# A newly searched order of 1751 steps in a two-layer transformer kernel

## The chip, the cores and the metric

The kernel runs on one core of one Trainium2 chip. The metric is the device time of one execution in microseconds (us). The core has five engines that run beside each other, each through its own list of instructions in order: PE (TensorE, matrix products and transposes), DVE (VectorE), ACT (ScalarE), POOL (GpSimd) and SP (SyncE, which here only issues DMAs). They wait for each other by semaphores.

## The reference, cut to what matters

Input: eight sequences ("batches" b = 0 to 7) of 512 tokens by 256 features, in float32. Two layers, each an attention part and a feed part, each part fed by a normalised, scaled and shifted input and added back through a gate:

```python
# layer 0
h = layernorm(x) * (1 + ca) + sa
x = x + ga * (h + concat(lin(h), win(h)) @ Wout)   # lin: linear attention on a feature map; win: softmax over a window of 64
h = layernorm(x) * (1 + cb) + sb                    # then mixed with the token before it
x = x + gb * (sigmoid(xr @ W_r) * (square(relu(xk @ W_k)) @ W_v))
# layer 1
h = layernorm(x) * (1 + ca) + sa
x = x + ga * (causal_softmax_attention(rope(h)) @ w_proj + b_proj)
h = layernorm(x) * (1 + cb) + sb
h = silu(h @ w1.T) * (h @ w2.T)
h = gelu(h @ h1.T); h = gelu(h @ h2.T)
x = x + gb * (h @ w3.T)
```

Each attention has 16 heads of 16 features, handled in four "quads" of four heads. The feed part of layer 1 has 1024 hidden features and ternary weights.

## The kernel before

The work is cut into 1751 named steps, `layer:name.numbers`. One table, the string ORDER (L1201 on), lists them, and every engine runs its own part of each step in that listed order; a step in which an engine has no part costs it nothing. So the table fixes five instruction streams at once. The waits are worked out from the steps' names. The PSUM places are dealt out in the listed order too: in layer 0 `lin`, `win` and `wm` steps use the four "wide" banks, and most other steps take turns on two single banks, m0 and m1.

Steps of layer 0 (b is the batch, n = 4b + quad):

- `stats.b` statistics of x (DVE L542, and POOL L448 takes the power); `norm.b`, `rms.b` the normalised input h (`rms` also has SP load the next batch's norm gates); `hT`, `qk`, `v` transpose and project it; `tq.n`, `tk.n` turn queries and keys (DVE L695 keeps the low part of the queries), `fold.n` the feature map.
- `wm.n.0`, `pair.n` (= `wm.n.1` and `lin.n-1.2`) the window's maxima (DVE L705 to L714), `again.n` turns them back; `lin.n.j`, `win.n.j` the weights (PE into a wide fill, then an ACT activation L862, L869, then POOL masks L452, L457); `lv.n.j`, `wv.n.j` the products with the values (PE L1077); `lh.n`, `wh.n` turn the sums back (PE L1087) and divide them (DVE L562 to L567); `turn.b.i`, `out.b.i` the output product. `out.b.i` also has DVE add the result to x, take statistics and, with i = 1, write the second norm xn (L735), and has SP load the gate ga of batch b + 1 (L353).
- `xg.b` on POOL: h *= ga, x += h (L475, L476); it waits for that gate.
- `xT.b.i` turns xn (PE L971); with i = 1, DVE mixes it with the token before (L741, L744, two of each for r, two for k). `r.b.i` and `kk.b.i` are the products of the feed part. `last.b.i` is its last product (PE L1129) and the add into x (DVE L574, L575); SP writes half a batch to x_mid (L398), and after `last.b.1` waits for both halves and loads x of batch b + 3 into the same buffer (L401), which `stats.b+3` reads.
- `wt.i.half` prepares the weights of layer 1: DVE collects low bits (L588) and transposes (L593) a piece that lies in SBUF, SP writes it out (L372) and issues the loads of the piece after next, 16 small DMAs in most steps (L345), 8 in the first few (L350).

Steps of layer 1: `stats`, `norm`, `hT`, `proj` (PE L1908, DVE L1665 to L1678), `tq`, `tk` (PE L1917), `max.b.g.j` (three wide fills a quad, PE L1937; DVE adds the mask L1685 and takes the maxima L1688), `again` (L1924), `att.b.g.j` (PE L1951, L1955, ACT exp L1833 or its like, POOL mask L1607), `values` (L1971), `heads`, `turn`, `out`, `xT`, `split`, and the feed part `up`, `h1`, `h2`, `last` (PE L2012, L2028, L2042). The attention of batch b + 1 is laid between the feed steps of batch b. "The seam" below is the stretch in which the last batch of layer 0 and the first attention of layer 1 run together, before any feed step of layer 1 can be laid between.

Of the kernel before, what the change touches and what calls it, by code (L numbers as in the profile page):

```python
# [1201 lines left out]
0:stats.0 0:norm.0 0:wturn.0.0 0:mod0.0 0:hT.0.0 0:masks.0 0:hT.0.1 0:rows.0.0 0:rms.0 0:qk.0.0 0:qk.0.1 0:qk.0.2 0:wt.0.0 0:qk.0.3 0:v.0.0 0:tq.0  # L1202
0:xg.0 0:tk.0 0:wturn.0.1 0:wm.0.0 0:tk.1 0:tk.2 0:wturn.0.2 0:tq.1 0:pair.0 0:fold.0 0:fold.1 0:wt.0.1 0:wm.1.0 0:mod.0 0:lin.0.0 0:again.0 0:lin.0.1
0:v.0.1 0:pair.1 0:stats.1 0:wt.1.0 0:tq.2 0:lv.0.0 0:again.1 0:win.0.0 0:lv.0.1 0:fold.2 0:win.0.1 0:tq.3 0:lin.1.0 0:lv.0.2 0:wv.0.0 0:rows.0.1
0:wt.1.1 0:win.1.0 0:wv.0.1 0:tk.3 0:lv.1.0 0:norm.1 0:wm.2.0 0:hT.1.0 0:hT.1.1 0:wv.1.0 0:win.1.1 0:rms.1 0:lh.0 0:wh.0 0:wt.2.0 0:lin.1.1 0:qk.1.0
0:wv.1.1 0:pair.2 0:v.1.0 0:again.2 0:lin.2.0 0:fold.3 0:lv.1.1 0:wt.2.1 0:lin.2.1 0:qk.1.1 0:win.2.0 0:lv.1.2 0:qk.1.2 0:wm.3.0 0:qk.1.3 0:lv.2.0
0:pair.3 0:wt.3.0 0:tk.4 0:lh.1 0:wv.2.0 0:lin.3.0 0:wh.1 0:tq.4 0:lv.2.1 0:wt.3.1 0:win.2.1 0:again.3 0:lv.2.2 0:lin.3.1 0:tq.5 0:lh.2 0:win.3.0
0:wv.2.1 0:lv.3.0 0:fold.4 0:turn.0.0 0:wm.4.0 0:v.1.1 0:turn.0.2 0:pair.4 0:wv.3.0 0:tk.5 0:lv.3.1 0:win.3.1 0:wt.4.0 0:stats.2 0:fold.5 0:lv.3.2
0:lin.4.0 0:wh.2 0:wv.3.1 0:lh.3 0:again.4 0:lin.4.1 0:wh.3 0:turn.0.1 0:turn.0.3 0:wt.4.1 0:wm.5.0 0:out.0.0 0:pair.5 0:out.0.1 0:tk.6 0:win.4.0
0:lv.4.0 0:xg.1 0:tq.6 0:lv.4.1 0:win.4.1 0:again.5 0:lv.4.2 0:lin.5.0 0:wt.5.0 0:fold.6 0:tq.7 0:win.5.0 0:lh.4 0:wv.4.0 0:lin.5.1 0:wv.4.1 0:tk.7  # L1210
0:xT.0.0 0:norm.2 0:wm.6.0 0:hT.2.0 0:hT.2.1 0:lv.5.0 0:rms.2 0:pair.6 0:wh.4 0:qk.2.0 0:wt.5.1 0:again.6 0:lin.6.0 0:wt.6.0 0:wv.5.0 0:lv.5.1
0:xT.0.1 0:lv.5.2 0:win.5.1 0:qk.2.1 0:lin.6.1 0:qk.2.2 0:lv.6.0 0:win.6.0 0:fold.7 0:qk.2.3 0:wm.7.0 0:tk.8 0:r.0.0 0:tq.8 0:pair.7 0:v.2.0 0:wv.5.1
0:lv.6.1 0:win.6.1 0:lh.5 0:again.7 0:lv.6.2 0:lin.7.0 0:wh.5 0:tk.9 0:wv.6.0 0:wt.6.1 0:wv.6.1 0:lin.7.1 0:kk.0.0 0:fold.8 0:win.7.0 0:kk.0.1 0:tq.9
0:win.7.1 0:lv.7.0 0:lh.6 0:wm.8.0 0:lv.7.1 0:v.2.1 0:pair.8 0:r.0.1 0:again.8 0:wv.7.0 0:lv.7.2 0:win.8.0 0:wh.6 0:wt.7.0 0:last.0.0 0:wv.7.1
0:lin.8.0 0:last.0.1 0:lh.7 0:wm.9.0 0:turn.1.2 0:turn.1.0 0:wv.8.0 0:wh.7 0:tq.10 0:lin.8.1 0:turn.1.1 0:wt.7.1 0:lv.8.0 0:turn.1.3 0:tq.11 0:pair.9
0:fold.9 0:out.1.0 0:lin.9.0 0:wt.8.0 0:out.1.1 0:lin.9.1 0:lv.8.1 0:tk.10 0:win.8.1 0:again.9 0:tk.11 0:wm.10.0 0:lv.8.2 0:xg.2 0:xT.1.0 0:fold.10
0:wv.8.1 0:lh.8 0:pair.10 0:stats.3 0:lv.9.0 0:lv.9.1 0:xT.1.1 0:lin.10.0 0:again.10 0:lv.9.2 0:win.9.0 0:r.1.0 0:win.9.1 0:lv.10.0 0:win.10.0
# [956 lines left out]
```

## Time and profile before

| | |
|---|---|
| median of 3 runs | 1990.87 us (1989.52 to 1991.04) |
| profiled execution, its own time | 1990.24 us |
| its span, first to last instruction | 1988.5 us |
| PE busy | 1866.2 us (94%) |
| DVE, ACT, POOL busy | 68%, 45%, 26% |
| mean granted clock of PE | 0.972 |
| chain that ended last | PE 74%, DVE 14%, ACT 5%, issue 3% |

The profile gives busy time by engine; what an engine waited for; a timeline; and windows with the granted clock of PE (1.00 is 2.4 GHz, 0.50 is 1.2 GHz). A row of the timeline is: start in us from the start of the span, duration in us, engine, line, operation, tiles written and read, shapes, number of merged instructions, and in brackets the idle time of the engine before it and what ended it.

### The profile page before, as it was taken

Reading aid. Unit: us, or ns where it says so; the run is one execution under the profiler, and the core shown is the slowest. Engines: PE = TensorE matmul, PEld = TensorE weight load, DVE = VectorE, ACT = ScalarE, POOL = GpSimd, SP = SyncE. Lnnn points to the kernel's source line nnn. Section 1 sums busy time; section 2 is a strip of 40 time slices with the busy share of each in tenths; the row PEclk is TensorE's granted clock in tenths of the full one; section 3 lists DMA queues with packets and bytes.
Section 4 is the critical chain, followed back from the end, with each engine's and each line's share of the span. In section 5 each row is a group of like instructions: output and inputs, shape, how many; then the busy total and the mean of one; then the engine's idle time right before and its main releaser. Section 6 shows DMA issues by size and latency. Waiting matters only on the chain.

```text
span 1988.5 us, 40531 instructions
## 1 busy us (share of the span) xinstructions
PE 1866.2 (94%) x16217; PEld 1308.3 (66%) x16217; DVE 1359.8 (68%) x2382; ACT 904.1 (45%) x1134; POOL 509.0 (26%) x597
## 2 busy tenths in 40 slices
...
DMA packets 171818, 126.36 MB, mean 64 GB/s; under 512 B 113944, under 2 KB 148720, under 8 KB 171248
## 3 DMA queue, kind: packets, MB, share of 16 engines
...
q8 instruction: 133, 2.18, 0.5%
q14 instruction: 53, 0.43, 0.1%
q10 hardware_dynamic: 832, 0.01, 0.0%
...
## 4 chain that ended last, share of the span: by engine, by line
PE 74%; DVE 14%; ACT 5%; issue 3%; SPq 1%; POOL 1%; DMA 1%; DVEq 0%; ACTq 0%; POOLq 0%
PE ps L2028 24%; PE ps L2012 4%; PE ps L1077 4%; PE ps L1908 3%; PE ps L1971 3%; PE ps L982 3%; PE ps L2042 3%; PE ps L1937 3%; DVE b_maxima L1688 3%; PE ps L1951 2%; PE ps L1107 2%; PE ps L1955 2%; PE ps L1040 2%; PE ps L1022 2%; PE ps L1129 2%
## 5 line engine op out<-in xcount | busy, mean ns | idle before, releaser
L2028 PE MATMUL ps<-b_acts,b_hidden_w 128*128 128x512 f32 x2048 | 504.4, 399 | 0.7 <-DVEq L1769 0.7
L2028 PEld LDWEIGHTS ps<-b_acts,b_hidden_w 128*128 128x128 f32 x2048 | 376.3, 188 | 92.1 <-issue 12.9
L452 POOL TENSOR_SCALAR_AFFINE_SELECT a_probs<-a_probs 128x512 f32<-128x512 f32 (+1 forms) x224 | 166.1, 757 | 374.0 <-ACT a_probs L862 249.5
L1607 POOL TENSOR_SCALAR_AFFINE_SELECT b_work<-b_work 128x512 f32<-128x512 f32 x128 | 82.4, 657 | 659.6 <-ACT b_work L1833 659.5
L862 ACT ACTIVATE a_probs<-ps 128x2048 f32<-128x2048 f32 (+1 forms) x96 | 153.1, 1595 | 141.6 <-DVEq L712 104.8
L1865 ACT ACTIVATE b_acts_exact<-ps,c_s 128x512 f32<-128x512 f32 x128 | 88.2, 689 | 273.6 <-PE ps L2028 273.3
L1833 ACT ACTIVATE b_work<-ps 128x2048 f32<-128x2048 f32 (+1 forms) x96 | 153.3, 1596 | 88.5 <-PE ps L1955 87.0
L1688 DVE TENSOR_REDUCE b_maxima<-ps 128x4 f32<-128x2048 f32 (+3 forms) x128 | 187.8, 1488 | 3.3
L1778 DVE CAST b_acts<-b_acts_exact 128x512 fp32r<-128x512 f32 x128 | 60.5, 473 | 166.0 <-ACT b_acts_exact L1865 165.7
L1077 PE MATMUL ps<-a_probs,c_va 128*17 128x192 f32 (+4 forms) x2048 | 134.3, 380 | 4.7 <-issue 2.2
L1685 DVE TENSOR_TENSOR ps<-ps,c_causalr 128x512 f32<-128x512 f32 x128 | 86.1, 695 | 43.3 <-PE ps L1937 41.6
L1615 POOL TENSOR_TENSOR b_acts<-b_acts_exact,b_acts 128x512 fp32r<-128x512 f32 x64 | 82.3, 1285 | 126.9 <-DVE b_acts L1773 126.9
L1937 PE MATMUL ps<-c_k_split,c_q_split 32*128 32x512 f32 (+3 forms) x1024 | 68.0, 362 | 25.8 <-DVE b_maxima L1688 13.6
L1779 DVE TENSOR_TENSOR b_acts<-b_acts_exact,b_acts 128x512 fp32r<-128x512 f32 x128 | 88.6, 692 | 4.4
L1971 PE MATMUL ps<-b_work,c_va 128*17 128x512 f32 (+3 forms) x1024 | 87.5, 450 | 2.4 <-POOL b_work L1607 2.4
L1908 PE MATMUL ps<-c_wqkv,b_work 128*128 128x512 f32 (+1 forms) x256 | 85.9, 487 | 0.4 <-ACTq L876 0.4
L1077 PEld LDWEIGHTS ps<-a_probs,c_va 128*17 128x17 f32 x2048 | 46.9, 97 | 58.7 <-issue 43.1
L1937 PEld LDWEIGHTS ps<-c_k_split,c_q_split 32*128 32x128 f32 x1024 | 42.0, 190 | 60.0 <-issue 23.1
L1861 ACT ACTIVATE b_acts_exact<-ps,c_s 128x512 f32<-128x512 f32 x64 | 44.0, 688 | 82.0 <-PE ps L2012 80.3
L2012 PE MATMUL ps<-b_acts,b_w1T 128*128 128x512 f32 x256 | 74.4, 412 | 4.8 <-DVEq L1769 4.1
L1951 PEld LDWEIGHTS ps<-b_shift,c_shift_rows 32*128 32x128 f32 x1280 | 46.3, 184 | 45.8 <-issue 21.0
L2012 PE MATMUL ps<-b_acts,b_w2T 128*128 128x512 f32 x256 | 75.6, 418 | 0.6 <-DVEq L1786 0.6
...
## 6 DMA issues: line engine op xcount, KB each, us to landing
b_hidden_w<-turned_h SPq DMA_DIRECT2D x128, 512.0 KB, 3.5
a_raw_next<-in_L_ffn_h_w SPq DMA_DIRECT2D x512, 16.0 KB, 1.8
...
```

The lines of the kernel that those rows point to most:

```text
L452: return nc.gpsimd.affine_select(out=z, in_=z, compare_op=ALU.is_ge, fill=0.0, base=0, pattern=[[0, blocks_n], [1, cols]], channel_multipl ...
L862: nc.scalar.activation(pb, here[:, :, o:o + w], ACT.Square, bias=1.0, scale=0.5).then_inc(att_ready, 1)
L1077: ins = nc.tensor.matmul(here[R * i:R * i + HD + 1, kb * P:kb * P + q], va[:, b % 2, kb, 4 * g + i, :], pb[:, first + i * pitch:first + i ...
L1688: ins = nc.vector.tensor_reduce(maxima[:, t, :].unsqueeze(2), room["wide"][:, :, o:o + (t + 1) * P], AX.X, ALU.max, negate=True)
L1779: nc.vector.tensor_tensor(dst[:, 1], z, dst[:, 0].bitcast(F32), ALU.subtract).then_inc(h_split, 1)
L1833: ins = nc.scalar.activation(probs[nth % 2][:, 0:4 * w].rearrange("p (h q) -> p h q", q=w), here[:, :, 0:w], ACT.Exp, scale=float(HD) ** -0.5)
L1865: nc.scalar.activation((exact_a if name == "h2" else exact_b)[:, m], here, ACT.Gelu, scale=s12[:, 2 + (name == "h2"), m:m + 1]).then_inc(g ...
L1908: ins = nc.tensor.matmul(here[:, a, 0:w], hT[:, k, t * P:(t + 1) * P], wqkv[:, k, o:o + w], start=(k == 0), stop=(k == ND - 1))
L1937: ins = nc.tensor.matmul(here[:, i, o:o + (t + 1) * P], part[rows_of(i), g % 2, t * P:(t + 1) * P], ksplit[rows_of(i), g % 2, 0:(t + 1) * ...
L1971: ins = nc.tensor.matmul(room["acc"][R * i:R * i + HD + 1, kb * P:S], va[:, kb, 4 * g + i, :], probs[nth % 2][:, i * w + o:i * w + o + S - ...
L2012: ins = nc.tensor.matmul(here, view((w1T, w2T)[j][:, i, k]), view(h2r[:, k, part]), start=(k + part == 0), stop=(k == ND - 1 and part == 1))
L2028: ins = nc.tensor.matmul(here, view(hidden_w[:, m, k]), view(src[:, k, i]), start=(k + i == 0), stop=(k == NHID - 1 and i == 1))
```

## The change

The string ORDER is replaced by another listing of the same 1751 steps. No operation, no wait and no buffer is changed; only the places of steps in the list (and with them which of m0 and m1 a step of layer 0 gets). The steps from `1:xT.7` on stand as before. 127 lines of the table differ; two of them, those around the load of the fifth batch:

```diff
@@ -1199,133 +1199,133 @@
...
-0:last.1.0 0:lin.11.1 0:wt.9.1 0:last.1.1 0:wh.10 0:wm.12.0 0:tk.13 0:turn.2.2 0:lv.11.0 0:fold.12 0:tq.13 0:pair.12 0:wv.11.0 0:lh.10 0:v.3.0
...
+0:wt.9.1 0:tk.12 0:win.11.0 0:wv.10.1 0:last.1.0 0:tk.13 0:wm.12.0 0:lv.11.0 0:lv.11.1 0:fold.12 0:tq.13 0:win.11.1 0:wv.11.0 0:lh.10 0:pair.12
+0:wh.10 0:last.1.1 0:fold.13 0:wm.13.0 0:wv.11.1 0:again.12 0:turn.2.2 0:lv.11.2 0:wh.11 0:turn.2.0 0:lin.12.0 0:lh.11 0:v.3.0 0:wt.10.0 0:win.12.0
...
```

Place 1, SP, around `last.1.0` and `last.1.1`. Before: the write-out and the loads of `wt.9.0`, the first half of x, `wt.9.1` with its 16 loads, the second half and the load of batch 4.

```order
L372 DMA turned_h<-a_staged 128x512
L345 DMA a_raw_next<-in_L_ffn_h_w 32x4x32 x16
L398 DMA x_mid<-a_x 128x2x256
L372 DMA turned_h<-a_staged 128x512
L345 DMA a_raw_next<-in_L_ffn_h_w 32x4x32 x16
L398 DMA x_mid<-a_x 128x2x256
L401 DMA a_x<-in_L_attn_x 128x4x256
```

Now:

```order
L372 DMA turned_h<-a_staged 128x512
L345 DMA a_raw_next<-in_L_ffn_h_w 32x4x32 x16
L372 DMA turned_h<-a_staged 128x512
L345 DMA a_raw_next<-in_L_ffn_h_w 32x4x32 x16
L398 DMA x_mid<-a_x 128x2x256 x2
L401 DMA a_x<-in_L_attn_x 128x4x256
```

Both `wt` steps now stand ahead of both halves, and the load of batch 4 follows the second half at once.

Place 2, POOL, around `xg.4` (L475, L476). Before, the mask of `lin.17.2` (the one L452 row right above) stands ahead of it:

```order
L448 TENSOR_TENSOR a_rstd<-a_vareps,c_minus_half 128x4
L452 AFFINE_SELECT a_probs<-a_probs 128x4x128 x4
L457 AFFINE_SELECT a_probs<-a_probs 128x4x128
L452 AFFINE_SELECT a_probs<-a_probs 128x4x128
L475 TENSOR_TENSOR a_h<-a_h,a_ga 128x1024
L476 TENSOR_TENSOR a_x<-a_x,a_h 128x1024
L452 AFFINE_SELECT a_probs<-a_probs 128x8x128
```

Now `xg.4` is ahead of that mask, and so earlier:

```order
L448 TENSOR_TENSOR a_rstd<-a_vareps,c_minus_half 128x4
L452 AFFINE_SELECT a_probs<-a_probs 128x4x128 x2
L457 AFFINE_SELECT a_probs<-a_probs 128x4x128
L452 AFFINE_SELECT a_probs<-a_probs 128x4x128 x2
L475 TENSOR_TENSOR a_h<-a_h,a_ga 128x1024
L476 TENSOR_TENSOR a_x<-a_x,a_h 128x1024
L452 AFFINE_SELECT a_probs<-a_probs 128x4x128 x2
```

`xg.3` goes the other way. Before, it stands behind the masks of `win.12.1` (L452 x4 and L457), ahead of that of `lin.13.2`:

```order
L452 AFFINE_SELECT a_probs<-a_probs 128x4x128 x4
L457 AFFINE_SELECT a_probs<-a_probs 128x4x128
L475 TENSOR_TENSOR a_h<-a_h,a_ga 128x1024
L476 TENSOR_TENSOR a_x<-a_x,a_h 128x1024
L452 AFFINE_SELECT a_probs<-a_probs 128x4x128
L452 AFFINE_SELECT a_probs<-a_probs 128x8x128
```

Now the mask of `lin.13.2` is the last of the three rows merged above it:

```order
L452 AFFINE_SELECT a_probs<-a_probs 128x4x128 x2
L457 AFFINE_SELECT a_probs<-a_probs 128x4x128
L452 AFFINE_SELECT a_probs<-a_probs 128x4x128 x3
L475 TENSOR_TENSOR a_h<-a_h,a_ga 128x1024
L476 TENSOR_TENSOR a_x<-a_x,a_h 128x1024
L452 AFFINE_SELECT a_probs<-a_probs 128x4x128
```

So `xg.3` now starts right ahead of `xT.2.1`, in the same pattern (`pair`, `wh`, `wt`, `xT.b.1`) in which `xg.4` stood before.

Place 3, PE, the first attention quad of layer 1 in the seam. L1937 x8 of 512 columns is `max.0.0.0`, the next two L1937 rows are `max.0.0.1`. Before:

```order
L1040 MATMUL ps<-a_mT,c_k_split 128x256 x8
L1937 MATMUL ps<-c_k_split,c_q_split 128x512 x8
L1937 MATMUL ps<-c_k_split,c_q_split 128x384 x8
L1937 MATMUL ps<-c_k_split,c_q_split 128x128 x8
L1917 MATMUL ps<-c_identr,c_nat 128x128 x4
L1077 MATMUL ps<-a_probs,c_va 17x512 x4
L1917 MATMUL ps<-c_identr,c_nat 128x128 x4
L1077 MATMUL ps<-a_probs,c_va 17x384 x4
L1077 MATMUL ps<-a_probs,c_va 17x128 x4
L1937 MATMUL ps<-c_k_split,c_q_split 128x256 x8
L1937 MATMUL ps<-c_k_split,c_q_split 128x512 x8
```

Now:

```order
L1040 MATMUL ps<-a_mT,c_k_split 128x256 x8
L1937 MATMUL ps<-c_k_split,c_q_split 128x512 x8
L1917 MATMUL ps<-c_identr,c_nat 128x128 x8
L1077 MATMUL ps<-a_probs,c_va 17x512 x4
L1937 MATMUL ps<-c_k_split,c_q_split 128x384 x8
L1937 MATMUL ps<-c_k_split,c_q_split 128x128 x8
L1129 MATMUL ps<-a_wrT,a_mix 128x256 x4
L1937 MATMUL ps<-c_k_split,c_q_split 128x256 x8
```

Between the first and the second fill of that quad now stand two turns (L1917) and one product with values (L1077) where nothing stood; between the second and the third stands one product (L1129) instead of two turns and three products.

## Rows read from the trace of the kernel before

**Rows 1.** The page: busy us of each engine, share of the span, instructions.

```profile
PE 1866.2 (94%) x16217; PEld 1308.3 (66%) x16217; DVE 1359.8 (68%) x2382; ACT 904.1 (45%) x1134; POOL 509.0 (26%) x597
```

**Rows 2.** Windows: length, busy PE, PEld, DVE, ACT, POOL, clock, DMA share, GB/s.

```profile
100.00:700.00 600.00, 564.79 (x6182) 374.11 (x6181) 417.88 (x750) 350.46 (x463) 243.01 (x289) 0.97 0.22 51
700.00:1000.00 300.00, 254.90 (x2390) 164.22 (x2392) 214.88 (x369) 123.30 (x142) 72.36 (x89) 0.93 0.13 45
1000.00:1900.00 900.00, 886.19 (x6619) 650.11 (x6620) 635.23 (x1067) 371.90 (x441) 153.67 (x166) 1.00 0.25 73
```

**Rows 3.** Timeline of the DMA queue around the fifth batch's load: start, us, what.

```profile
310.05 8.41 SPq L345 DMA_DIRECT2D a_raw_next<-in_L_ffn_h_w  x16
318.50 0.43 SPq L398 DMA_DIRECT2D x_mid<-a_x  x1
320.71 0.39 SPq L401 DMA_DIRECT2D a_x<-in_L_attn_x  x1
```

**Rows 4.** Timeline of DVE and of POOL: first instruction behind a transfer.

```profile
324.65 1.41 DVE L542 BATCH_NORM_STATS2 a_stats<-a_x 128x6 f32<-128x256 f32 x4 [4.86 <-DMA a_x<-in_L_attn_x]
...
417.79 1.41 DVE L542 BATCH_NORM_STATS2 a_stats<-a_x 128x6 f32<-128x256 f32 x4 [3.18 <-DMA a_x<-in_L_attn_x]
...
259.56 2.37 POOL L475 TENSOR_TENSOR a_h<-a_h,a_ga 128x1024 f32<-128x1024 f32 x1 [5.03 <-DMA a_ga<-gate_rows]
```

**Rows 5.** Timeline of PE behind those three transfers.

```profile
265.06 1.05 PE L1077 MATMUL ps<-a_probs,c_va 128*17 128x256 f32 x8 [2.09 <-POOL a_probs L452]
...
327.39 0.66 PE L1087 MATMUL ps<-c_identr,a_sums 128*128 128x128 f32 x4 [1.33 <-DVEq L684]
...
331.68 1.06 PE L1077 MATMUL ps<-a_probs,c_va 128*17 128x192 f32 x24 [1.36 <-issue]
...
420.70 0.66 PE L1087 MATMUL ps<-c_identr,a_sums 128*128 128x128 f32 x4 [1.71 <-DVE a_onat L567]
```

**Rows 6.** Timeline of POOL and of DVE, collision of the fourth batch.

```profile
455.77 2.38 POOL L475 TENSOR_TENSOR a_h<-a_h,a_ga 128x1024 f32<-128x1024 f32 x1
455.85 5.08 DVE L741 TENSOR_SCALAR a_mix<-a_xT,a_one_mu 128x512 f32<-128x512 f32 x2
```

**Rows 7.** Timeline of DVE, the same work undisturbed, and the other collision.

```profile
754.74 0.88 DVE L741 TENSOR_SCALAR a_mix<-a_xT,a_one_mu 128x512 f32<-128x512 f32 x2 [0.73 <-ACT a_xT L898]
...
634.68 2.03 DVE L735 SCALAR_TENSOR_TENSOR a_xn<-a_x,a_meanvar,a_rstd 128x256 f32<-128x256 f32 x4 [1.12 <-POOL a_rstd L448]
...
539.96 4.90 DVE L735 SCALAR_TENSOR_TENSOR a_xn<-a_x,a_meanvar,a_rstd 128x256 f32<-128x256 f32 x4 [1.12 <-POOL a_rstd L448]
...
544.78 2.83 DVE L588 SCALAR_TENSOR_TENSOR a_lows<-a_raw_next,a_lows 128x512 int32<-128x512 int32 x1
```

**Rows 8.** Timeline of PE at both collisions.

```profile
452.37 0.66 PE L1087 MATMUL ps<-c_identr,a_sums 128*128 128x128 f32 x4
...
463.60 2.90 PE L1129 MATMUL ps<-a_wrT,a_mix 128*128 128x256 f32 x6 [4.14 <-DVE a_mix L744]
...
548.86 1.12 PE L971 MATMUL ps<-c_identr,a_xn 128*128 128x128 f32 x4 [4.20 <-DVE a_qlow L695]
```

**Rows 9.** Windows at the lower clock, columns as in rows 2.

```profile
264.60:271.20 6.60, 6.14 (x51) 4.66 (x52) 5.08 (x8) 2.52 (x3) 3.27 (x4) 0.50 0.01 2
421.60:424.80 3.20, 3.20 (x44) 2.41 (x44) 0.88 (x4) 1.43 (x2) 1.07 (x2) 0.50 0.18 28
547.90:554.50 6.60, 5.58 (x34) 4.01 (x38) 4.86 (x8) 1.36 (x2) 0.79 (x2) 0.50 0.27 65
```

**Rows 10.** Timeline of PE at the seam: four stalls.

```profile
789.00 1.33 PE L1937 MATMUL ps<-c_k_split,c_q_split 32*128 32x384 f32 x16 [3.13 <-DVE b_maxima L1688]
...
853.01 0.55 PE L1951 MATMUL ps<-b_shift,c_shift_rows 32*128 32x128 f32 x12 [2.03 <-ACTq L1836]
...
895.46 0.66 PE L1917 MATMUL ps<-c_identr,c_nat 128*128 128x128 f32 x4 [2.65 <-DVE c_nat L1678]
...
936.30 0.51 PE L1937 MATMUL ps<-c_k_split,c_q_split 32*128 32x256 f32 x8 [2.18 <-DVE b_maxima L1688]
```

More of the change, by code:

```diff
@@ L1201 @@
 ORDER = """
[L1202 to L1217, printed above, removed]
```

235 lines of the change are left out of this document (125 added, 110 removed).

## The prediction

> **What bounds the kernel now.** I read the busy times of the page first: PE is busy for 1866.2 of 1988.5 us [rows 1]. No operation changes, so its work stays. What an order can move is the rest, 122 us, and the stretches in which PE runs at the lower clock. Then the windows by stage: layer 0 (100 to 700 us) has PE idle for 600 - 564.8 = 35.2 us at a mean clock of 0.97; the seam (700 to 1000) for 300 - 254.9 = 45.1 us at 0.93; the 900 us after it for 13.8 us at 1.00 [rows 2]. So the long stage in which feed steps fill every hole has nothing to give, and setup and tail stand nearly as before. The place to look is layer 0 and the seam. Next, the waits that end on a DMA, then the timeline of PE for every idle time over 1 us, each followed back to what was late. Three causes show in layer 0.
>
> First, transfers that were issued late. The load of batch 4 should follow the second half of x to x_mid. SP had just begun the 16 small loads of `wt.9.1`, which took 8.41 us of its time; the half went out at 318.50 and the load at 320.71 [rows 3]. DVE, which meets `stats.4` in its fixed order, then stood idle for 4.86 us; the same with batch 5, 3.18 us; and POOL waited 5.03 us for a gate ga behind the loads of `wt.8.0` [rows 4]. On PE this came out as 2.09, then 1.33 + 1.36, then 1.71 us of idle time [rows 5].
>
> Second, collisions of POOL and DVE. While POOL ran `xg.4` (its first half, L475, 2.38 us), the first two L741 of the mix took 5.08 us [rows 6]; alone they take 0.88 [rows 7]. `r.3.0` came 4.14 us late on PE [rows 8]. In batch 4 `xg.5` met xn: four L735 took 4.90 us in place of 2.03, and the L588 behind them 2.83 [rows 7]; `tq.23`, behind that, gave its bank back late, and `xT.4.0` waited 4.20 us [rows 8].
>
> Third, the clock: behind three of these stalls the granted clock is 0.50 (1.2 GHz) for 6.6, 3.2 and 6.6 us, with PE busy before them at 1.00 (2.4 GHz) up to the stall [rows 9].
>
> **The change part by part.** It removes and adds nothing and moves nearly everything a little. The two lists have the same shape: each batch's projections, output products and feed steps begin within some 15 us of PE work of their old places. I therefore price only the places that stalled, and those that have become thinner than places that stalled.
>
> 1. Transfers. In the new order no `wt` with 16 loads stands within 9 us of PE work ahead of any `last.b.1` or `out.b.1`; before, the nearest stood 2 to 4 us ahead in the three cases above. `stats.b` now stands 17 us of PE work or more behind the step that frees its buffer (before, 11.0 and 11.6 in the two cases that stalled; out of the queue it needs the 2.2 us between 318.50 and 320.71 and 3.9 to the landing before 324.65 [rows 3, 4]). Moved past SP's other work, the `wt` steps come no closer to each other than 12 us for the same half, against 8.41 for its loads. So these waits go: 2.09 + 1.33 + 1.36 + 1.71 = 6.5 us. Bounds: 0 if other waits stand right behind them, 13.1 if the whole of DVE's and POOL's idle time (4.86 + 3.18 + 5.03) comes back. I take 6.5, which PE itself shows.
>
> 2. Collisions. `xg.5` now also has the mask of `lin.21.1` and the power of `stats.6` ahead of it on POOL, so it starts some 3 us later, behind xn: minus 4.2 us. `xg.4` is now ahead of `lin.17.2` and runs before the mix: minus 4.1 us. But `xg.3` has been moved behind the mask of `lin.13.2` and `wt.11.1`, exactly the pattern in which `xg.4` collided. From the product before (`wh.16` at 452.37) to `r.3.0` at 463.60 were 11.2 us, 4.14 of them idle [rows 8]; the new list has the same steps there but for one turn and one short product, less one turn, some 0.6 us less work, so `r.2.0` should wait 4.14 + 0.6 = 4.7 us. Net of the three: -4.2 - 4.1 + 4.7 = -3.6 us. Bounds: -8.3 (the new collision does not come) and +0.6 (`xT.4.0` still waits).
>
> The two engines met within 0.1 us of each other (455.77 and 455.85) [rows 6], and the one that came second paid. The Trainium skill (SBUF — State Buffer, "Who interferes with whom") says that the shared pair of ports is an exclusive lock and that issue order, not the operation, decides who blocks. By that, in the new place DVE may as well win, and then POOL would wait for 0.4 us and PE for nothing; this is one reason for a rival below.
>
> 3. Clock. The three stretches at 0.50 are 16.4 us long [rows 9]. Work that runs at half speed there would take half of it, so at most 8.2 us come back; their PE rows are not all limited by the clock, and other holes may set off others. I take half, 4.1 us. Bounds 8.2 back and 3.3 lost (one more stretch of 6.6 us). The one behind `r.3.0` I let move to `r.2.0`.
>
> 4. The seam. With nothing between `max.0.0.0` and `max.0.0.1`, PE waited 3.13 us for DVE's maxima [rows 10]; now 2 us of work stand there: -2.0. `att.0.0.1` now follows `att.0.0.0` at once; where that was so before, it cost 2.03 us [rows 10]: +2.0. Between a second and a third max fill (2.18 us idle with 2.1 us of work between [rows 10]) six places of layer 1 now have at most 2.5 us of work, before four: two more at some 2 us: +4.0 (the fill right behind the one just named is one of them, 1.9 us in place of 3.0). A first and second fill of the third quad have 2.2 us between them in place of 4.3: +1. The first `tk` of batch 1 (2.65 us idle [rows 10]) has 0.9 us more ahead of it: -1.0. Sum +4. Bounds -5 (the old stalls there merge with new ones) and +13 (all six thin fills pay in full, in a row).
>
> 5. Everything else. By the same tally a handful of pairs elsewhere in both layers are thinner than any that ran free before: `values.4.0.2` 0.9 us behind its weights, three turns of sums 0.5 us behind their copies, `xT.3.0` and `xT.6.0` some 5 us behind `out`. I put 3 us on all; bounds 0 and 6.
>
> Sum: -6.5 - 3.6 - 4.1 + 4 + 3 = -7.2 us. Against the profiled execution's own 1990.24 us that is 1983.0; the median of the runs lies 0.6 us above it, so 1983.5.
>
> **The rivals.**
>
> A larger gain: DVE wins the port at `xg.3` or the two miss each other (-4.7), and the stalls of the seam only change places (-4): -7.2 - 8.7 = -15.9, 1975 us. For it: the times of the two engines there differ by less than I can tell. Against: the list repeats the old pattern, and the seam has real thin spots.
>
> No difference: the idle time is kept and only changes its place. DVE is busy for 418 of 600 us in layer 0 and 215 of 300 in the seam [rows 2], waits of different kinds lie side by side, and filling one takes work from another. Then of step 1 half remains, of the clock nothing: -3.3 - 3.6 + 4 + 3 = 0, 1990 us.
>
> Slower: the seam. A PE that waits for every max fill and every weights fill runs in bursts there; the clock of 0.93 over 300 us means 42 us of it at half speed already [rows 2]. If all six thin fills pay 2.2 us each (+13 in place of +4) and these holes keep the clock down for another 20 us (+10), the sum is -7.2 + 9 + 10 = +12, 2002 us; the point from which it decides is about 7 us of idle time and clock lost in the seam beyond my 4. For it: the clock there falls behind stalls of only 1 to 3 us. Against: the largest of them, 3.13 us, is filled.
>
> That the new list does not do what its name says I rule out: the SP rows show the loads out of the way.
>
> **How the numbers follow.** Chances: forecast 0.45 (own range 1978 to 1988), larger gain 0.19, no difference 0.20, slower 0.16. What a measurement of this kernel can tell from no change is 0.2%, 4 us: faster means under 1986.9. Of the forecast 0.41 lies there, all of the larger gain, 0.02 of the third: 0.62. Within 4 us: 0.04 + 0.17 = 0.21. Slower: 0.16 + 0.01 = 0.17. The range 1970 to 1996 takes in the larger gain, no difference, and of the slower case its near part.
>
> **What would show it.** DVE has no idle time that ends on the load of a_x, POOL at most one, in the setup, on a_ga. No idle time of 4 us at `r.3.0` and `xT.4.0`; one of 4 to 5 at `r.2.0`, with an L741 pair of some 5 us beside L475. PE idle from 100 to 700 us at 26 us or less, from 700 to 1000 at 45 to 50, mean clock 0.975 or so. The forecast is wrong if the window from 700 to 1000 us holds 7 us more idle time or its clock falls under 0.90, or if layer 0 keeps its 35 us with other names on it.

## The result and the profile after

| | us, median | runs |
|---|---|---|
| before | 1990.95 | 20 |
| after | 1994.72 | 20 |

The ratio is 1.0022 (95% interval 1.0012 to 1.0032): slower by 0.22%, where 0.4% faster was forecast. The profiled execution of after took 1992.53 us, 2.2 us under the median of its runs, so what its trace shows of the loss (2.3 us against before's own 1990.24) is a little less than the loss of the medians. Every execution of every run below is counted but one: of run 14's twelve, one took 3645.85 us and is left out of its ratio.

Two details of the change: the table has 1750 entries, and behind `1:xT.7` two of them, `split.7` and `last.6.1.0`, have changed places too. Nothing below rests on either.

The busy line of the page, columns as in [rows 1]:

```profile
PE 1865.9 (94%) x16217; PEld 1305.2 (66%) x16217; DVE 1358.6 (68%) x2382; ACT 910.8 (46%) x1140; POOL 509.8 (26%) x597
```

PE's busy time is the same to 0.3 us. The windows, as in [rows 2], show that this sum hides two opposite changes:

```profile
100.00:700.00 600.00, 568.44 (x6310) 376.38 (x6310) 424.72 (x764) 353.84 (x467) 246.59 (x295) 0.99 0.21 49
700.00:1000.00 300.00, 251.26 (x2252) 162.57 (x2250) 212.24 (x356) 117.00 (x136) 67.57 (x83) 0.90 0.14 47
1000.00:1900.00 900.00, 884.25 (x6625) 646.88 (x6624) 628.30 (x1064) 378.77 (x445) 153.54 (x165) 1.00 0.25 73
```

Layer 0 has 31.6 us of PE idle time (35.2 before) and its mean clock rose from 0.97 to 0.99; the seam has 48.7 (45.1) and its clock fell from 0.93 to 0.90; the 900 us behind have 15.8 (13.8).

The transfers of [rows 3, 4] are out of the way. The timeline of the DMA queue at the load of batch 4, and the first work of DVE behind it, which has no idle time:

```profile
317.95 3.28 SPq L345 DMA_DIRECT2D a_raw_next<-in_L_ffn_h_w  x7
321.27 1.77 SPq L398 DMA_DIRECT2D x_mid<-a_x  x2
325.07 0.37 SPq L401 DMA_DIRECT2D a_x<-in_L_attn_x  x1
...
334.00 1.40 DVE L542 BATCH_NORM_STATS2 a_stats<-a_x 128x6 f32<-128x256 f32 x4
```

The collisions of [rows 6, 8] are gone at `xg.4` and `xg.5`, and the new one came at `xg.3` as worked out: POOL's L475 began 0.08 us ahead of DVE's pair of L741, which then took 5.06 us, and `r.2.0` waited 4.00 us on PE (4.7 forecast):

```profile
354.01 2.36 POOL L475 TENSOR_TENSOR a_h<-a_h,a_ga 128x1024 f32<-128x1024 f32 x1
354.09 5.06 DVE L741 TENSOR_SCALAR a_mix<-a_xT,a_one_mu 128x512 f32<-128x512 f32 x2
...
361.83 1.62 PE L1129 MATMUL ps<-a_wrT,a_mix 128*128 128x256 f32 x3 [4.00 <-DVE a_mix L744]
```

In the seam the thin fills wait as the four of [rows 10] did. The timeline of PE at `max.0.0.2`, `att.0.0.1`, `max.1.2.2` and, behind the seam, `max.2.2.2`:

```profile
789.43 0.51 PE L1937 MATMUL ps<-c_k_split,c_q_split 32*128 32x256 f32 x8 [1.87 <-DVE b_maxima L1688]
...
804.50 0.55 PE L1951 MATMUL ps<-b_shift,c_shift_rows 32*128 32x128 f32 x12 [2.03 <-ACTq L1836]
...
953.97 0.51 PE L1937 MATMUL ps<-c_k_split,c_q_split 32*128 32x256 f32 x8 [1.68 <-DVE b_maxima L1688]
...
1094.31 0.51 PE L1937 MATMUL ps<-c_k_split,c_q_split 32*128 32x256 f32 x8 [2.34 <-DVE b_maxima L1688]
```

To compare two orders step by step I matched PE's instructions to the steps, and took from the time of a milestone (the end of a step that stands at nearly the same place in both lists) the nominal work of all steps listed before it, each step at the median of its kind in before. What is left is idle time and slowness (PE busy for longer than nominal). The slowness is an estimate, good to about 1 us. The last column is the time at 0.50 in the record of the granted clock:

| stretch | idle, before and after | slowness, before and after | clock at 0.50 |
|---|---|---|---|
| start to `last.5.1` (714 us) | 53.3, 50.2 | 9.4, 1.3 | 61.4, 40.9 |
| to `up.0.7.1` (965 us) | 44.7, 48.4 | 16.8, 24.7 | 40.9, 58.1 |
| to the last step | 18.7, 20.9 | 5.7, 5.6 | 6.8, 3.4 |

(The clock's column is by time: up to 700 us, 700 to 1000, and from 1000 to PE's last instruction.) Layer 0 won 11.2 us, 8.1 of them slowness; the second stretch lost 11.6, 7.9 of them slowness; the rest lost 2.1. The second stretch is more than the seam. The experiments below cut the lists just ahead of `up.0.2.0` (some 930 us), where both have the same steps behind them: up to there the same reckoning gives a loss of 6.7 us (2.3 idle, 4.4 slowness), from there to `up.0.7.1` 5.1 (1.5 and 3.6). Time at 0.50 went down by 20.5 us, then up by 17.2, and half of such time is lost work: 10.2 and 8.6 us, beside 8.1 and 7.9 of slowness. So the clock accounts for the slowness in both stretches, and the idle time moved less. Over the whole kernel the two clock shares cancel: slowness 31.9 us before and 31.6 after, idle time 116.7 and 119.5.

### The profile page after: what moved, and what is told of

It reads as the page before. It is cut to its first block, busy times and chain, and to the rows that moved or that the text cites. A ratio compares the mean times of both kernels' runs of the same rounds, so it can differ in the third digit from the quotient of the medians.

```text
span 1990.8 us, 40537 instructions
## 1 busy us (share of the span) xinstructions
PE 1865.9 (94%) x16217; PEld 1305.2 (66%) x16217; DVE 1358.6 (68%) x2382; ACT 910.8 (46%) x1140; POOL 509.8 (26%) x597
## 4 chain that ended last, share of the span: by engine, by line
PE 78%; DVE 14%; ACT 4%; issue 2%; POOL 0%; DMA 0%; SPq 0%; DVEq 0%; ACTq 0%; POOLq 0%
PE ps L2028 24%; PE ps L2012 5%; PE ps L1077 4%; PE ps L1908 4%; PE ps L1971 3%; PE ps L982 3%; PE ps L2042 3%; PE ps L1937 3%; PE ps L1951 2%; PE ps L1955 2%; PE ps L1107 2%; PE ps L1022 2%; PE ps L1040 2%; DVE b_maxima L1688 2%; PE ps L1129 2%
## 5 line engine op out<-in xcount | busy, mean ns | idle before, releaser
L452 POOL TENSOR_SCALAR_AFFINE_SELECT a_probs<-a_probs 128x512 f32<-128x512 f32 (+1 forms) x224 | 166.2, 758 | 357.5 <-ACT a_probs L862 249.0
L1778 DVE CAST b_acts<-b_acts_exact 128x512 fp32r<-128x512 f32 x128 | 55.8, 436 | 171.9 <-ACT b_acts_exact L1865 171.6
L1077 PE MATMUL ps<-a_probs,c_va 128*17 128x192 f32 (+4 forms) x2048 | 135.3, 385 | 2.9 <-issue 1.6
L1685 DVE TENSOR_TENSOR ps<-ps,c_causalr 128x512 f32<-128x512 f32 x128 | 86.2, 696 | 50.2 <-PE ps L1937 48.2
L1937 PE MATMUL ps<-c_k_split,c_q_split 32*128 32x512 f32 (+3 forms) x1024 | 68.4, 363 | 29.5 <-DVE b_maxima L1688 13.6
L1077 PEld LDWEIGHTS ps<-a_probs,c_va 128*17 128x17 f32 x2048 | 47.9, 98 | 58.6 <-issue 39.8
L1937 PEld LDWEIGHTS ps<-c_k_split,c_q_split 32*128 32x128 f32 x1024 | 42.0, 191 | 62.9 <-issue 23.4
L457 POOL TENSOR_SCALAR_AFFINE_SELECT a_probs<-a_probs 128x1024 f32<-128x1024 f32 (+2 forms) x96 | 74.7, 794 | 4.4
```

The lines of the kernel that those rows point to most:

```text
L452: return nc.gpsimd.affine_select(out=z, in_=z, compare_op=ALU.is_ge, fill=0.0, base=0, pattern=[[0, blocks_n], [1, cols]], channel_multipl ...
L1077: ins = nc.tensor.matmul(here[R * i:R * i + HD + 1, kb * P:kb * P + q], va[:, b % 2, kb, 4 * g + i, :], pb[:, first + i * pitch:first + i ...
L1937: ins = nc.tensor.matmul(here[:, i, o:o + (t + 1) * P], part[rows_of(i), g % 2, t * P:(t + 1) * P], ksplit[rows_of(i), g % 2, 0:(t + 1) * ...
```

## The experiments

Each run is a re-listing of the same steps. "Old" is the list before, "new" the list after. Differences in us are differences of ratio times 1991; a single ratio is good to 0.1 or 0.2%, so a difference of two of these runs has some 3 to 5 us on either side.

**Runs 1 to 3: which stretch of the list loses.**

```diff
-new
+run 1: new[:722] + what is left, in old order
+run 2: new[:901] + what is left, in old order
+run 3: old[:722] + what is left, in new order
```

> The list is the new one up to the end of batch 5 (its first 722 entries, last step a first half of last.5), and the steps left stand in their old order: new layer 0, old seam, old layer 1. Theory A, the seam's own order is the loss: in the two profiles the new list is 11.2 us ahead at last.5.1, and from there the old order should keep it: 1991 - 11 = 1980 us, ratio 0.994 to 0.995; window 700:1000 with 43 to 47 us of PE idle time and a clock of 0.92 to 0.93, as before. Theory B, what layer 0 wins the seam gives back whatever its order (the granted clock there falls when more work was done before it, or the products of the seam wait for something that layer 0 does not move): 1990 to 1995 us, clock in the seam 0.90 or 0.91.

> The new list up to step up.0.1.1 of layer 1 (about 935 us), the old order behind it: it prices the new order of the long stage of layer 1 alone. Theory A: the profiles were 1.8 us apart in favour of the new one at 925 us and 2.5 us against it at the end, so the rest of the new list costs some 4 us: 1991 - 2 = 1989 us, ratio 0.999. Rival: that 4 us is run-to-run noise or a late effect of the seam and stays: 1994 us, as the whole new list, ratio 1.002.

> The reverse of the first: old order up to the end of batch 5 (722 entries), the steps left in their new order. Theory A (the loss lies in the new seam and the new layer 1): 1991 + 11 (what the seam lost by 1000 us) + 3 (behind it) = 2005 us, ratio 1.006 to 1.008; window 700:1000 with 48 us or more of PE idle and a clock of 0.90. Theory B (the loss is the answer to a faster layer 0): about 1991 us, ratio 1.000 to 1.001, with the seam's clock at 0.93.

Measured: run 1 1986.85 us, ratio 0.9976 (0.9964 to 0.9988); run 2 1987.12 us, 0.9976 (0.9966 to 0.9985); run 3 2005.6 us, 1.0072 (1.0057 to 1.0087). Run 3 is as theory A said: new seam and new layer 1 cost 14 us on an old layer 0, and since the whole new list stands at 1.0022, the new layer 0 is worth 10. Run 1 is between the theories. Its trace points to the reason: the lead of 9.8 us at `last.5.1` fell to 5.3 at `out.6.1`, at the joint of the two orders, where `win.28.1` and `win.29.0` waited 1.66 and 1.52 us as in neither list. A joint has a price of its own. Run 2 against the whole new list gives 9 us (give or take 3) for the new order behind 934 us; I had 4, and the trace of after shows 7 there. Runs 1 and 2 have the same ratio, so behind the new layer 0 the new seam cost nothing, or 4.5 us if run 1's joint is taken off; on a repaired old layer 0 it cost 7 (run 11).

**Run 4: the collision at `xg.3`, moved later.**

```diff
-0:xg.3 0:xT.2.1 0:lv.13.0 0:lin.14.0 0:lv.13.1 0:again.14 0:win.13.0 0:lh.12 0:r.2.0
+0:xT.2.1 0:lv.13.0 0:lin.14.0 0:lv.13.1 0:again.14 0:win.13.0 0:lh.12 0:r.2.0 0:xg.3
```

> The whole new list with one step moved: xg.3 stands behind r.2.0, and so behind the mix of xT.2 on DVE, in place of ahead of xT.2.1. Theory C, the collision of POOL's L475 with DVE's first L741 pair (5.06 us in the new profile, r.2.0 4.00 us late on PE, 3.4 us at the lower clock behind it) is what that place costs: r.2.0 has no idle time, the L741 pair takes about 0.9 us, -4.0 - 1.7 = -5.7: 1994.7 - 5.7 = 1989 us, ratio to the kernel before 0.999. Rival: POOL's two instructions of 4.8 us now meet other work of DVE (L665 of the next batch's h), which is stretched as much, and PE waits there: 1993 to 1995 us, ratio 1.001 to 1.002.

Measured: 1997.53 us, ratio 1.0031 (1.002 to 1.0042). The collision went (the first L741 pair took 0.84 us, `r.2.0` had no idle time) and a wait took its place, which neither theory named (the rival had `L665` stretched, not waiting). DVE's next norm writes a_h, and must wait until POOL has read it; in time order:

```profile
363.52 2.36 POOL L475 TENSOR_TENSOR a_h<-a_h,a_ga 128x1024 f32<-128x1024 f32 x1
365.96 2.37 POOL L476 TENSOR_TENSOR a_x<-a_x,a_h 128x1024 f32<-128x1024 f32 x1
368.44 3.53 DVE L665 SCALAR_TENSOR_TENSOR a_h<-a_x,a_meanvar,a_hg 128x256 f32<-128x256 f32 x4 [6.91 <-POOL a_x L476]
373.34 1.72 PE L971 MATMUL ps<-c_identr,a_h 128*128 128x128 f32 x4 [4.84 <-DVE a_h L669]
```

DVE stood idle for 6.91 us and `hT.4.0` on PE for 4.84, more than the 4.00 that had been won.

**Runs 5 to 7: the terms of the prediction, one by one, in the old list.**

```diff
 run 5
-0:wt.9.1 0:last.1.1            -0:wt.13.0 0:lin.15.1 0:last.2.1   -0:wt.8.0 0:out.1.1
+0:last.1.1 0:wt.9.1            +0:lin.15.1 0:last.2.1 0:wt.13.0   +0:out.1.1 0:wt.8.0
 run 6
-0:pair.18 0:xg.4               -0:xg.5 0:wt.17.1 0:lin.21.1
+0:xg.4 0:pair.18               +0:wt.17.1 0:lin.21.1 0:xg.5
 run 7: both
```

> The old list with three steps moved by a few places: wt.9.1 right behind last.1.1, wt.13.0 right behind last.2.1, wt.8.0 right behind out.1.1. So no step with 16 loads stands ahead of a load of a_x or of that of a_ga. It prices the first term of the prediction alone. Theory A (the waits go, nothing stands behind them): DVE's 4.86 and 3.18 us and POOL's 5.03 us of idle time gone; PE wins the 6.5 us of its own, and with the lower clock behind two of these stalls (6.6 and 3.2 us at 0.50, so up to 4.9) 6.5 to 11: 1991.5 - 8.5 = 1983 us, ratio 0.995 to 0.997. Rival (other waits stand right behind them): 0 to 2 us, ratio 0.999 to 1.000.

> The old list with two steps moved: xg.4 ahead of pair.18 (POOL idle there for 8 us), xg.5 behind lin.21.1, one mask later. It prices the removal of the two collisions alone. Theory A: r.3.0 and xT.4.0 lose their 4.14 and 4.20 us of PE idle time and the two stretches of 6.8 us at the lower clock behind them go (6.8): -8.3 - 6.8 = -15 us at most, 1991.5 - 12 = 1980 us, ratio 0.993 to 0.996. Rival: POOL's pair of 4.8 us meets other work of DVE that reads and writes SBUF only, as in the run in which xg.3 stood behind r.2.0 and another step waited 4.84 us: 0 to -5 us, ratio 0.998 to 1.001.

> The old list with both of the two edits before: five steps moved, all else as before. If the terms add, the gains of the two runs add up: 1991.5 - 8.5 - 12 = 1971 us, ratio 0.988 to 0.991, half-clock time between 400 and 700 us at 7 us or less against 23.9. If idle time only changes its place (the rival of no difference), the sum is less than the larger of the two: ratio 0.995 or above. The seam is in its old order, 700:1000 at a clock of 0.92 to 0.93: if it gives back what layer 0 wins whatever its order, the ratio is 0.996 or above too, and the lead at the end of layer 0 is 5 us or more larger than that at the end.

Measured: run 5 1980.36 us, ratio 0.9939 (0.9919 to 0.9959); run 6 1984.79 us, 0.9963 (0.995 to 0.9976); run 7 1975.31 us, 0.9923 (0.9903 to 0.9943). So the two repairs are worth 12, 7 and together 15 us: more, less and less than theory A had, and in no case what the rival had. Within their intervals the terms add, and five moved steps beat both kernels.

What came back was not the idle time. PE's window from 100 to 700 us in run 5 (columns as in [rows 2]):

```profile
100.00:700.00 600.00, 565.09 (x6244) 373.07 (x6244) 422.19 (x756) 355.37 (x466) 243.91 (x292) 0.98 0.22 51
```

PE is idle for 34.9 us, where before had 35.2: the waits of 2.09, 1.33 and 1.36 us are gone, as forecast, and waits of 3.75, 1.16 and 1.35 us have come: what the rival said of idle time, though not its price. The trace is 5.5 us ahead at `last.5.1` all the same, with 13.6 us less at 0.50. In run 7 the 14.2 us of lead there are 4.9 of idle time and 9.3 of slowness, where terms 1 and 2 for these places were 14.8 of idle time. In run 6 `xT.4.0` waited 0.75 us in place of 4.20, but `r.3.0` still 2.56: `xg.4` is earlier only as far as its gate's transfer allows. In run 7 the trace's lead was still 13.2 us at `up.0.7.1`. The old seam gives next to nothing back (5.5 and 5.4 in run 5, 6.3 and 6.6 in run 6), so theory B of run 1 has fallen.

Removing a wait can uncover a collision. In run 5 the gate for `xg.2` came in time, POOL started earlier, beside DVE's xn, and the L588 behind it took 2.86 us; in time order:

```profile
253.03 3.15 DVE L735 SCALAR_TENSOR_TENSOR a_xn<-a_x,a_meanvar,a_rstd 128x256 f32<-128x256 f32 x4 [1.13 <-POOL a_rstd L448]
255.88 2.54 POOL L475 TENSOR_TENSOR a_h<-a_h,a_ga 128x1024 f32<-128x1024 f32 x1
256.11 2.86 DVE L588 SCALAR_TENSOR_TENSOR a_lows<-a_raw_next,a_lows 128x512 int32<-128x512 int32 x1
...
261.89 0.69 PE L1022 MATMUL ps<-a_bandr,c_identr 128*128 128x192 f32 x4 [3.75 <-DVE a_maxima L707]
```

PE waited 3.75 us there, where 2.09 had been [rows 5].

**Run 8: a place for `xg.3` that works.** On the list of run 2:

```diff
-0:pair.14 0:wh.12 0:wt.11.1 0:xg.3      -0:xT.6.0 0:lv.29.2
+0:xg.3 0:pair.14 0:wh.12 0:wt.11.1      +0:lv.29.2 0:xT.6.0
```

> The list of the second run (new up to 920 us, old behind it) with two steps moved: xg.3 ahead of pair.14, one mask earlier, when the new norm has been long read and the mix has not begun; xT.6.0 behind lv.29.2, 1.1 us later. If the collision at r.2.0 (4.00 us of idle time, 3.4 to 6.8 us at the lower clock) goes without the wait of the next norm that cost the gain in the fourth run: -4 - 2.5; at xT.6.0 the idle time of 1.96 us halves and with it the 6.8 us at the lower clock: -1 to -4. Sum some -8: 1987 - 8 = 1979 us, ratio 0.993 to 0.995. Rival (POOL's pair delays the masks that lh.12 and the feed's products wait for by 2 to 4 us): ratio 0.997 to 0.998, as the second run.

Measured: 1979.71 us, ratio 0.9945 (0.9926 to 0.9964), against 0.9976 for run 2, so -6 us; I had -8. `r.2.0` on PE:

```profile
359.57 2.90 PE L1129 MATMUL ps<-a_wrT,a_mix 128*128 128x256 f32 x6 [1.43 <-DVE a_mix L744]
```

The wait is down from 4.00 to 1.43 us. The other edit did not do what I expected: the lower clock behind `xT.6.0` lasted 6.8 us as before.

**Run 9: the price of a thin fill, ten times.** A fill is thin when too little work of PE stands ahead of it to cover what it waits for. On the list of run 7, for example:

```diff
-1:max.2.0.1 1:tk.2.1 1:h2.0.3.1 1:h2.0.4.0 1:max.2.0.2
+1:max.2.0.1 1:h2.0.3.1 1:max.2.0.2 1:tk.2.1 1:h2.0.4.0
```

> The list of the seventh run (old with five steps moved, ratio 0.9923) with ten third max fills of layer 1 put forward: in the quads 0 and 3 of batches 2 to 6 one product of the feed, 2.0 us, is left between max.b.g.1 and max.b.g.2, where 2.7 to 5.1 us stood. All ten lie between 1000 and 1700 us, where PE has no idle time of that kind and runs at 1.00. It prices a thin fill. Theory D (idle time and clock): each waits about 1.9 us as the thin fills of the new list did (1.68, 1.78, 1.87, 2.03, 2.34 us), and behind most of them the granted clock is 0.50 for 3.4 us, 1.7 us more: 10 x 3.6 = 36 us at most, 1975 + 25 to 36 = 2000 to 2011 us, ratio 1.004 to 1.009. Rival (idle time only): 1975 + 19 = 1994 us, ratio 1.001 to 1.002, mean clock 0.977 or more, as the seventh run.

Measured: 2001.89 us, ratio 1.0056 (1.0041 to 1.007): 26.5 us more than run 7, which is theory D and excludes the rival's 19. All ten fills waited, nine of them 1.77 or 1.78 us and one 1.63. The timeline of PE at the first and the last, and the windows around them (length, busy PE, clock, DMA share, GB/s):

```profile
1023.88 0.51 PE L1937 MATMUL ps<-c_k_split,c_q_split 32*128 32x256 f32 x8 [1.77 <-DVE b_maxima L1688]
...
1684.25 0.51 PE L1937 MATMUL ps<-c_k_split,c_q_split 32*128 32x256 f32 x8 [1.77 <-DVE b_maxima L1688]
```

```profile
1022.00:1030.00 8.00, 6.23 (x38) 1.00 0.21 66
1682.00:1690.00 8.00, 6.23 (x27) 0.79 0.11 18
```

The same stall left the clock at 1.00 once, and set it to 0.50 for 3.4 us the other time. From `up.0.7.1` to the last step, idle time rose by 16.7 us and slowness by 8.8, with 17 us more at 0.50, in five stretches of 3.4. Only three of the five stretches stood behind thin fills; two stood behind stalls of 1.39 and 1.75 us which run 7 has too, without a drop. So a stall of 1.77 us cost (16.7 + 8.8) / 10 = 2.6 us on the mean; a third of the price is the clock, and the stall alone does not say where it falls.

**Runs 10 and 11: the two parts of the new list on a clean one.** On the list of run 7:

```diff
+run 10: run 7[:901] + what is left, in new order
+run 11: run 7[:722] + entries 722 to 900 in new order + the rest in old order
```

> The list of the seventh run for its first 901 entries (up to step up.0.1.1 of layer 1, some 920 us), the new order behind it. It prices the last part of the new list with a layer 0 and a seam that are clean. In the profile of the new list this part lost 4.3 us against before, 2.34 of them at max.2.2.2, 1.57 and 1.68 at again.1.1 and max.1.2.2. Theory A (local): 1975 + 4 to 7 = 1980 us, ratio 0.994 to 0.996. Rival (the part costs nothing by itself): 1975 us, ratio 0.992 to 0.993.

> The list of the seventh run, but with its entries 722 to 900 in their new order (some 715 to 920 us); behind them the old order again. It prices the new seam alone, with its thin fills. In the traces with the new seam this stretch lost 9 to 12 us against the old one, 5 of them from xT.6.0 to hT.0 and 4 between max.0.2.2 and att.0.3.2, half as idle time, half as time at the lower clock. Theory A (local): 1975 + 10 = 1985 us, ratio 0.996 to 0.998, half-clock time between 700 and 1000 us 50 us or more against 44 in the seventh run. Rival (the first and the second run had the same ratio, so the new seam costs nothing): 1975 to 1977 us, ratio 0.992 to 0.993.

Measured: run 10 1984.14 us, ratio 0.9954 (0.9937 to 0.9971), 6 us over run 7; run 11 1981.98 us, 0.9959 (0.9941 to 0.9977), 7 us over it. Each part costs by itself (each difference has 5 us on either side), and their sum of 13 agrees with run 3's 14. The windows 700:1000 of run 7 and of run 11 (columns as in [rows 2]):

```profile
700.00:1000.00 300.00, 255.31 (x2331) 164.31 (x2330) 215.59 (x366) 121.22 (x143) 70.48 (x85) 0.93 0.14 47
```

```profile
700.00:1000.00 300.00, 253.84 (x2294) 164.28 (x2293) 212.25 (x359) 121.06 (x141) 71.19 (x84) 0.91 0.14 47
```

By steps, from `last.5.1` to `up.0.7.1`, run 11 had only 1.4 us more idle time than run 7 (45.8 and 44.4), but 5.3 us more slowness (23.3 and 18.0), and 54.7 us at 0.50 in place of 44.4. The new seam hardly waits longer, it waits at other places. Over all traces, the time at 0.50 between 700 and 1000 us was 41 to 44 us in the eight that have the old seam behind an old or repaired layer 0 (54.6 in run 1), and 55 to 68 in the whole new list and runs 3, 4, 11 and 14. But run 2 had 48 and run 8, also with the new order up to 934 us, only 38: one profile of one list does not fix it.

**Run 12: the one repair that the new seam made, alone.** On the list of run 7:

```diff
-1:max.0.0.0 1:max.0.0.1 1:tk.0.1 0:lv.31.0
+1:max.0.0.0 1:tk.0.1 0:lv.31.0 1:max.0.0.1
```

> The list of the seventh run with max.0.0.1 moved behind lv.31.0: 2 us of work between the first and the second max fill of the first quad, where nothing stood and PE waited 3.13 us. It is the one repair that the new seam made, alone. Theory A: idle time of 3.13 us gone, at max.0.1.0 perhaps 0.5 more, one stretch of the lower clock (6.8 us) shorter: 1975 - 3 to - 5 = 1971 us, ratio 0.990 to 0.991. Rival (DVE's chain of maxima bounds the whole quad, the idle time only moves on to max.0.0.2 and max.0.1.0): 1975 us, ratio 0.992 to 0.993, with idle times there of 2 us and more.

Measured: 1976.22 us, ratio 0.9922 (0.9906 to 0.9939), the same as run 7: the rival. The timeline of PE at `max.0.0.1`, `max.0.0.2` and `max.0.1.0`:

```profile
778.75 0.80 PE L1937 MATMUL ps<-c_k_split,c_q_split 32*128 32x384 f32 x16 [1.56 <-DVE b_maxima L1688]
783.34 0.80 PE L1937 MATMUL ps<-c_k_split,c_q_split 32*128 32x256 f32 x8 [2.21 <-DVE b_maxima L1688]
786.26 1.23 PE L1937 MATMUL ps<-c_k_split,c_q_split 32*128 32x512 f32 x8 [2.12 <-DVEq L1693]
```

3.13 us at the first became 1.56 there and 2.21 at the second, and a wait of 1.15 us at `max.0.1.1` went. From `max.0.0.1` to `max.0.1.1` that makes 5.9 us of idle time, where run 7 has 6.4: a filler here shifts the wait, because DVE's maxima bound the quad.

**Runs 13 and 14: what was open.**

```diff
 run 13, on run 7: wt.8.0 back
-0:out.1.1 0:wt.8.0
+0:wt.8.0 0:out.1.1
 run 14, on the whole new list: xg.3 as in run 8, and
-1:max.1.2.2 1:values.1.1.1 1:up.0.5.1 1:att.1.1.2 1:again.1.2 1:up.0.6.0 1:up.0.6.1
+1:values.1.1.1 1:up.0.5.1 1:att.1.1.2 1:max.1.2.2 1:up.0.6.0 1:up.0.6.1 1:again.1.2
-1:max.2.2.2 1:up.1.3.1 1:tk.2.3 1:up.1.4.0 1:again.2.2 1:values.2.1.2 1:ga.2 1:up.1.4.1
+1:up.1.3.1 1:tk.2.3 1:up.1.4.0 1:max.2.2.2 1:values.2.1.2 1:ga.2 1:up.1.4.1 1:again.2.2
```

> The list of the seventh run with wt.8.0 back in its old place (four steps moved in place of five). There the load of a_ga for xg.2 comes late again. Theory E (that wait was cover: without it POOL's L475 starts at 251.7 us beside DVE's xn and the L588 behind it takes 2.85 us, so wm.10.1 waits 3.73, win.9.0 1.15 and wh.8 1.35 us where only lv.9.2 had waited 2.09): 6.2 - 2.1 = 4 us less idle time, 1975 - 4 = 1971 us, ratio 0.990 to 0.991, one stall of 2 us at lv.9.2 again. Rival (the wait and the collision cost the same): 1975 us, ratio 0.992 to 0.993.

> The whole new list with five steps moved: xg.3 ahead of pair.14 (as in the eighth run), and the two thin fills behind 934 us filled: max.1.2.2 behind att.1.1.2, max.2.2.2 behind up.1.4.0, with again.1.2 and again.2.2 a little later. Theory A (the losses are these places): -6 for the collision (ratios 0.9945 against 0.9976 in the eighth and second run, less a little for xT.6.0), -1.7 - 2.3 of idle time and 3 of 3.4 us stretches at the lower clock, -5: 1995 - 6 - 9 = 1980 to 1984 us, ratio 0.995 to 0.997. Rival (the loss behind 934 us is spread over the stage, not in these two fills): only the collision's 4 to 6 us come back: 1989 to 1991 us, ratio 0.999 to 1.000.

Measured: run 13 1975.9 us, ratio 0.993 (0.991 to 0.9951), no different from run 7: the rival again. The trace does show the stalls change as theory E said (`lv.9.2` 2.25 us, 0.36 at `wm.10.1` for 3.73), and idle time up to `last.5.1` is 3.6 us less, but the time at 0.50 there is 3.4 us more, and the medians are the same within what six executions tell. Run 14 1993.38 us, ratio 1.0013 (0.9999 to 1.0026): theory A has fallen, and the run cannot be told from the new list itself. The timeline of PE behind the fill that I moved, at `up.1.4.0` and `again.2.2`:

```profile
1092.46 1.19 PE L2012 MATMUL ps<-b_acts,b_w1T 128*128 128x512 f32 x4 [1.43 <-DVEq L1769]
...
1097.98 0.30 PE L1924 MATMUL ps<-c_identr,c_kT 128*128 128x128 f32 x1 [2.21 <-DVE c_kT L1697]
```

The 2.34 us at `max.2.2.2` are gone, and 1.43 + 2.21 have come. Moving a late step later made the step that follows it thin. Nor did the whole of run 14 show the 6 us of run 8: its trace is 3 us ahead of after's at `last.5.1`, and level with it at the end.

## Why the prediction was wrong

Its steps, against what was measured:

1. Transfers, -6.5 us. All three waits went, with no DVE idle time on a_x. Alone in the old list they were worth 12 us (run 5, interval 8 to 16), 8 in its trace: the sum of terms 1 and 3 there. Right in that the waits went; wrong in what came back, since run 5's idle time in layer 0 is the same and its whole gain there is slowness. That it came to more than 6.5 was not worked out.

2. Collisions, -3.6 net. `xg.4` and `xg.5` free, `r.2.0` 4.00 us late for 4.7. Right in mechanism, place and size of the stalls. The loser was again the engine that came second, by 0.08 us, so the doubt from the Trainium skill (SBUF — State Buffer, "Who interferes with whom": an exclusive lock, issue order decides) was to the point, and here the trace agrees with the rule: the order had POOL first. Each of the two L741 lasted until one of POOL's two instructions was over (they took 2.56 and 2.57 us and ended at 356.66 and 359.15, POOL's at 356.37 and 358.87), so the price is that of POOL's pair.

3. Clock, -4.1. In layer 0 the slowness fell by 8.1 us. I had counted the three stretches at 0.50 that followed the stalls of terms 1 and 2 (16.4 us); in the whole of layer 0 there were 34.1 us from 100 to 700, and 17.0 are left. Mis-sized by half. By luck this made up for idle time: of the 10 us of terms 1 and 2 only 3.1 came back, since `fold.6` (2.91), `wm.26.1` (2.30), `win.4.1` (2.03) and some of 1.2 us are new or longer. That is term 5, too small for layer 0. Together: -11.2 measured, where terms 1 to 3 say -14.2 and the share of term 5 some +1.5.

4. The seam, +4. This is the step that failed. The sum of idle time was right, +3.7 measured, and the thin fills paid 1.68 to 2.34 us as priced, though not all of its parts were mine: beside the named ones, `max.1.0.1` (2.88), `tq.1.0` (1.96) and `xT.6.0` (1.96) wait as before did not, and the gain of 3.13 us at `max.0.0.1` is a shift when made alone (run 12). But I let the stalls cost their idle time alone: the clock was a term of layer 0 only, with no entry in the seam, where I wrote "the old stalls there merge with new ones". Up to `up.0.7.1` slowness rose by 7.9 us, 4.4 of them ahead of `up.0.2.0`. Run 9 measured what was left out: a stall of 1.77 us costs 2.6. Run 11 showed it in the seam itself, on a clean list: 7 us, in its trace 1.4 of idle time and 5.3 of slowness.

5. Everything else, +3. Behind `up.0.7.1` the trace lost 2.1 us, behind `up.0.2.0` 7. The medians of run 10 say 6 for that longer part, with 5 us on either side, and run 2 against after says 9, with 3. Some 4 of the thin fills of term 4 (`max.1.2.2`, `max.2.2.2`) fall there too, so term 5 was too small by a few us, part of it again slowness (3.5 of the 7).

In sum the seam and what lies behind it cost 14 us (run 3), where terms 4 and 5 had some 5.5 of their 7 for them, against 10 to 11 won in layer 0. The rival "slower: the seam" had the mechanism: it put 20 us more at 0.50 there, a loss of 10, and 17.2 came, a loss of 7.9 with the rest of the slowness. Its idle time (13) was too much, mine (4) was right. With its clock and my idle time the sum of the prediction would have been -7.2 + 10 = +2.8 us, near the +2.3 of the trace, though only because the errors of item 3 cancel. Its chance of 0.16 was too low. The test that the prediction named, 7 us more idle time in the window or a clock under 0.90, was not met (3.6 us and 0.90), and the forecast was wrong all the same. The other threshold, named with the rival, did hold: 7 us of idle time and clock together beyond my 4 in the seam; measured were 11.6, so 7.6 beyond.

The mean clock that every timed execution records says much the same without a trace. Each 0.001 of it is at most 2.0 us (all of it lost work), and 1.4 by the slope over 72 timed runs of the kernel before. The means below are good to 0.001 or better.

| compared | mean clock | of it clock, us | in all, us |
|---|---|---|---|
| before, run 3 | 0.9720, 0.9687 | 5 to 7 lost | 14 lost |
| run 3, after | 0.9687, 0.9728 | 6 to 8 won | 10 won |
| before, run 5 | 0.9720, 0.9767 | 7 to 9 won | 12 won |
| run 7, run 9 | 0.9772, 0.9725 | 7 to 9 lost | 26.5 lost |
| run 7, run 11 | 0.9772, 0.9756 | 2 to 3 lost | 7 lost |
| run 7, run 10 | 0.9772, 0.9766 | 1 lost | 6 lost |
| run 1, run 2 | 0.9734, 0.9750 | 2 to 3 won | 0 |
| run 2, after | 0.9750, 0.9728 | 3 to 4 lost | 9 lost |

So some half of what the new seam and the new layer 1 cost together is clock, and most of what the new layer 0 wins; for the seam alone the clock's part is less in the timed runs than in run 11's trace, and behind the new layer 0 (run 1 to run 2) it is not seen.

Open stays why the new seam's stalls are mostly followed by more of the lower clock than the old ones' at nearly equal idle time, and by how much: the traces go from 38 to 68 us, and no run isolates a feature of the order that decides it. Nor is it settled how the 14 us divide between the seam and what lies behind it (7 and 6 on run 7's list, 7 and 7 in the trace of after, none to 4.5 and 9 by runs 1 and 2), nor what in the order makes the part behind 934 us: run 14's two repairs did not return it.
